# GpSimd's wait for TensorE's sum in the last group of a tile: ahead of the first gather instead of ahead of the fifth

## The reference

```
hh = (x @ W).reshape(n, 8, 32)                      # x is layer-normed
scores = leaky_relu(s_src[src] + s_dst[dst])        # 206250 edges, sorted by dst
e = exp(scores - m[dst]);  alpha = e / denom[dst]
out = segment_sum(hh[src] * alpha, dst)             # per node, 256 wide
x = x + elu(layernorm(out + x))
x = x + moe(layernorm(x))                           # top 2 of 16 experts, 256-512-256, layernorm
```

## Time and profile before

| | |
|---|---|
| median of three runs | 3359.55 us |
| span of the profiled execution, first to last instruction | 3356.0 us |
| edge loop, about 150 to 2740 us of the span | POOL busy 1558 us of 2590 |
| in it | DVE busy 1345, PE 1219, ACT 740 us |
| one gather | 0.948 us busy, next one 0.30 us later |

### The profile page before, as it was taken

How to read it: one execution, slowest core, us unless ns; L and a number is a source line. 1 busy time by engine, 2 the same in 40 slices (tenths; PEclk the granted TensorE clock), 3 DMA queues, 4 the chain that set the end, 5 groups by cost and what they waited for, 6 DMA issues and landing times. The chain is left out here.

```text
span 3356.0 us, 43456 instructions
## 1 busy us (share of the span) xinstructions
PE 1788.4 (53%) x9190; PEld 1461.1 (44%) x9191; DVE 1682.9 (50%) x3940; ACT 1018.8 (30%) x2031; POOL 1847.4 (55%) x1944
## 2 busy tenths in 40 slices
PE   6243544545444454544545444454544535999985
PEld 5133433434333343433434333343333434898974
DVE  7454554645445454554645545454554542333346
ACT  4232323233232332323223232332323312333442
POOL 2456656666565665656666565665656523555520
PEclk9676777767777776777777777777777767999987
DMA  5443434434343343443434343343433336333343
GB/s 185 115 122 96 123 112 113 118 105 122 105 123 117 105 119 105 124 115 107 119 105 124 106 121 115 107 120 102 125 117 107 118 82 202 101 102 102 106 158 120
DMA packets 179756, 393.55 MB, mean 117 GB/s; under 512 B 52144, under 2 KB 100576, under 8 KB 173448
## 3 DMA queue, kind: packets, MB, share of 16 engines
q0 software_dynamic: 93984, 273.52, 28.5%
q1 hardware_dynamic: 69512, 105.33, 10.1%
q10 hardware_dynamic: 16224, 14.30, 1.6%
HBM read 356.52 MB, written 36.47 MB: 117 GB/s over the span
## 5 line engine op out<-in xcount | busy, mean ns | idle before, releaser
L1265 POOL DMA_INDIRECT gat<-table,idx x1632 | 1546.7, 948 | 996.0 <-issue 448.7
L1362 PE MATMUL ps_sum<-msg,hot 128*128 128x264 f32 x3332 | 1075.0, 492 | 1051.4 <-DVE msg L1409 793.1
L1362 PEld LDWEIGHTS ps_sum<-msg,hot 128*128 128x128 f32 x3332 | 814.4, 250 | 1253.9 <-issue 1069.4
L1409 DVE TENSOR_TENSOR msg<-gat,ps_weight 128x2304 f32<-128x2304 f32 x196 | 473.4, 2415 | 401.3 <-ACT ps_weight L1321 392.5
L1560 DVE TENSOR_TENSOR num<-acc,ps_sum 128x264 f32<-128x264 f32 x49 | 21.0, 429 | 692.2 <-remote 681.2
L1277 ACT ACTIVATE hotT<-dst_row,neg_id 128x4352 bf16<-128x4352 int16 x48 | 188.3, 3922 | 283.1 <-remote 255.1
L1679 ACT ACTIVATE std<-var 128x1 f32<-128x1 f32 x49 | 9.9, 203 | 832.3 <-DVE var L1571 832.3
L1406 DVE TENSOR_TENSOR hot<-ps_own,rel 128x1152 f32<-128x1152 f32 x196 | 251.0, 1280 | 0.0
L1348 PE MATMUL ps_look<-dst_split,hotT 128*128 (+1 forms) x1666 | 80.2, 191 | 276.9 <-ACT hotT L1279 264.2
L2089 PE MATMUL ps_ht<-xT,w_t 128*128 128x128 f32 x1712 | 213.4, 278 | 3.6 <-issue 1.7
L2089 PEld LDWEIGHTS ps_ht<-xT,w_t 128*128 128x128 f32 x1712 | 201.8, 194 | 7.9 <-issue 4.3
(11 more groups left out here) (397 smaller groups left out, 2056.5 us busy)
## 6 DMA issues: line engine op xcount, KB each, us to landing
dst_row<-dst_half SPq DMA_DIRECT2D x49, 1088.0 KB
gat<-table,idx POOLq DMA_INDIRECT x1666
b_t<-in_L_ffn_b_dram ACTq DMA_DIRECT2D x107, 128.0 KB
w_sb<-in_L_ffn_w_dram SPq DMA_DIRECT2D x6, 2048.0 KB, 12.4
listing<-list_f SPq DMA_DIRECT2D x736, 0.5 KB
back<-chosen SPq DMA_DIRECT2D x5, 1792.0 KB, 7.6
table<-rows SPq DMA_DIRECT2D x49, 128.0 KB, 1.7
y_rows<-y SPq DMA_DIRECT2D x49, 128.0 KB
```

What stands on the lines that cost most here:

```text
L1265: pool.indirect_dma_start(gat[:, GSTART[g] + k, :], None, table, bass.IndirectOffsetOnAxis(ap=idx[g][:, k:k + 1], axis=0)).then_inc(landed ...
L1362: last = pe.matmul(ps_sum[:, 0:SUM], hot[:, m, k, :], msg[:, m, k, :], start=(g == 0 and k == 0), stop=(g == NG - 1 and k == n - 1))
L1409: dve.tensor_tensor(msg[:, m, 0:n, 0:D].rearrange("p j (h d) -> p j h d", d=HD), gat[:, j:j + n, 0:D].rearrange("p j (h d) -> p j h d", d=HD),
```

## The change

In g3 of every tile, GpSimd's wait for `sum_done` of g3 of the tile before stands ahead of the first of the eight gathers, where it stood ahead of the fifth. g0 to g2 keep theirs.

```diff
                     for k in range(GROUPS[g]):
-                        if k == GROUPS[g] // 2:
+                        if k == (0 if g == NG - 1 else GROUPS[g] // 2):
                             pool.wait_ge(sum_done, (t - 1) * NG + g + 1)
                             pool.sem_inc(pool_turn, 1)
                         pool.indirect_dma_start(gat[:, GSTART[g] + k, :], None, table,
```

## The result

The changed kernel is 0.4% faster: median 3347.42 us of 10 runs against 3359.34 us of 10 runs of the kernel before, ratio 0.9961, 95% interval 0.9944 to 0.9978. The forecast was 3421 us, slower. The profiled execution has a span of 3342.4 us, 13.6 less than before.

The account below looks back on a forecast made before the run. Bound: a chain of waits through g3's signal, held until GpSimd stops. Terms of -5.0, +3.65, +0.2, +5.2 and -2.9 gave about 1.3 us per tile, over 47 tiles 61 us: 3421 us, range 3270 to 3515.

Parts of the forecast that it names:

- step 5: SyncE's list DMAs crawl, so `dst_row` goes out late in every tile: `hotT` +5.2 us, g3's signal no longer held -2.9.
- Reading of the bound: VectorE's wait at each tile's start: g3's sum is signalled only once GpSimd stops, 3.0 us after its last gather's end.
- Step 1: Four gathers leave the time ahead of g3's signal, so VectorE goes on earlier: a gain of 5.0 us per tile.
- Rival (C): g3's signal comes when TensorE is done, whatever GpSimd does: +172, 3531 us; chance 0.13, shared with results beyond the forecast.
- Step 2: On GpSimd the four moved gathers run behind the tile's start with g0's first four: twelve in a row, costing nothing themselves.
- Step 3: g0's sum falls amid twelve gathers in a row, so its signal is held: a cost of 3.65 us per tile.
- Rival (B): g0's sum isn't held: 4.6 us less per tile, 3144 us, or 3250 with half of it; chance 0.10.
- Step 4: From g1's gathers through `hotT` to g3's sum, adding 0.2 us: a tile takes 51.8 us, 1.1 less than 52.9.
- rival (A): SyncE issues its lists and `dst_row` in time, so step 5 is void: -52, 3308 us; chance 0.25.
- (D): The terms cancel, or the moved wait is passed at once: time within 0.2%; chance 0.12.

Follow-up runs that it names:

- e3: The changed kernel with the wait for g3's sum at g3's third gather instead of the first: 3292.33 us (one run), against 3364.7 us for the kernel before.
- e7: e1 with the wait for g3's sum at g3's third gather instead of the first: 3266.84 us, ratio 0.970 to the kernel before.
- e11: e7 with GpSimd's wait for g3's sum taken out: 3650.68 us (one run), against 3391.13 us for the kernel before.
- e6: The kernel before with `dst_row` issued ahead of the lists and one of eight matmuls left in g3's sum: 3270.53 us (one run), against 3364.7 us.
- e1: The changed kernel with `dst_row` issued ahead of the 16 list DMAs instead of behind them: 3274.25 us, ratio 0.9675 to the kernel before.
- e2: The kernel before with only `dst_row` issued ahead of the list DMAs: 3387.0 us, ratio 1.0002.
- e12: e7 with GpSimd's waits for the sums of all four groups taken out: 3928.42 us (one run), against 3391.13 us for the kernel before.
- e5: The kernel before with gathers of g2 and g3 fetching 64 bytes a row instead of 1088: 3399.57 us (one run), against 3384.21 us.
- e8: e7 with a fill of a scratch tile on GpSimd ahead of g1's and g3's first gather: 3467.07 us, ratio 1.0318 to the kernel before.
- e9: e7 with a fill of a scratch tile on GpSimd ahead of g3's first gather alone: 3259.76 us, ratio 0.9695 to the kernel before.

## Why the prediction was wrong, point by point

The forecast was 61 us more, measured are 12 us less. The step that failed is step 5, the count of SyncE's lists; the others were right in kind, with sizes off by up to 1 us.

**Reading of the bound: right for this kernel, too narrow as a rule.** The sum's signal comes some 3 us after GpSimd stops: S + 14.3 with the wait at the fifth gather, S + 11.5 at the third (e3, e7), S + 8.7 at the first, S + 20.2 with none (e11). But the 3 us aren't fixed (the last section has the counts), and e6 has signals that are late with no stop at all.

**Step 1: right.** S + 9.2 was forecast, 8.7 measured: L1560 at 1051.22 with the stop at 1048.64, a gain of 5.6 us against 5.0, since 2.6 us lie between stop and L1560 and not 3.1. Rival (C) falls with it, with e3 and with e6.

**Step 2: right.** Twelve gathers run without a pause, 1001.38 to 1016.08, T + 15.4 as forecast.

**Step 3: right in kind.** g0's sum is held: L1703 at T + 17.7 in both tiles, forecast T + 18.55, T + 15.1 if not held. The fifth gather of g0 starts at T + 18.4 instead of T + 19.35, a cost of 2.7 us for 3.65. Rival (B) falls.

**Step 4: right.** `hotT` at T + 31.5 and S at T + 41.8, forecast T + 32.3 and T + 42.6. The first tile above takes 50.5 us, forecast 51.8 for a tile with `dst_row` in time: 0.5 us of that is step 1's, the rest step 3's.

**Step 5: wrong.** Its single tile was met: `dst_row` at T + 31.6 (forecast T + 33), `hotT` at T + 38.2 (37.5), S at T + 48.5 (47.9), T = S + 6.6 (6.3), a tile of 55.1 (54.2). What failed is that I let every tile be late. The step starts its count with 1 to 2 lists out before T, which holds where the sum is held up. But the late tile it arrives at ends with a prompt sum beside a quiet GpSimd, and there the lists go out 1.26 us apart and five are out before T. By the step's own count the next tile then has 5 + 6 + 2 to 3 + 4 = 17 or 18 lists of time for 16, and is in time, as measured: `dst_row` at T + 25.4. I had written this very argument for rival (A) and gave it 0.25 instead of carrying the late tile's end state into the next count. The mean of 50.5 and 55.1 is 52.8, 0.1 us below before, where the step had +1.3; over 47 tiles these 1.4 us are 66 of the 74 us between forecast and result. With the alternation, the prediction's own prices of 51.8 and 54.2 us give a mean of 53.0: so 1.2 of the 1.4 us are the step's error, and 0.2 are sizes that were off either way and partly cancel, which is luck. The 5.2 us ahead of the first L1560, which a sum over 47 tiles left out, are most of the rest.

**The rivals.** (A) priced a kernel in which SyncE is in time, 3308 us, 1.5% faster; e1, which makes it so, is 3.2% faster, so (A) was priced too high (on e1's chip a tile went from e2's 53.5 to 51.1 us, where (A) had 1.1 us less). The result lies between (A) and the forecast because the tiles do. (D), "the terms cancel", comes nearest to the time, though not within 0.2%.

## What to carry to other kernels

When a step's sum ends in a different state from the one it began with, it has to be run a second time from that state: the alternation would have come out of the prediction's own numbers, as 51.8 and 54.2 us and about no change (measured 50.5 and 55.1). When a change removes hundreds of us of waiting and the time hardly moves, look for the instruction whose idle time is new in the costliest groups; here it was one DMA queued behind sixteen small ones, and moving it turned 0.4% into 3.2%. Before a wait that protects nothing is taken out, ask what gets done while its engine stands still: here it cost 8 us per tile to remove one.

## What the hardware showed that was not expected

Beside unbroken gathers of GpSimd (one per 1.25 us), TensorE's signals reach VectorE, ScalarE and GpSimd late: in the kernel before and most others 2 to 5 us after GpSimd stops, in 13 of 45 tiles of e6 while it goes on. In e11 the signal of a 5.4 us sum comes 20.2 us after the sum's start, in its first tile 28.4 us. The delay is longer the longer GpSimd has gone without a pause. Counted over the tiles whose sum is held up until after the stop (a pause is over 0.6 us; the times are medians and run to L1560's start):

| gathers since the last pause | from stop to L1560, us |
|---|---|
| 13 | 2.6 (after), 2.8 (e1) |
| 15 | 2.8 (e7), 2.9 (e3) |
| 16 | 3.4 (e12) |
| 17 | 3.1 (before), 3.3 (e2) |
| 21 | 4.0 (e11) |
| 26 | 4.4 (before, first two tiles) |
| 30 | 5.2 (e11, first two tiles) |

Kernels with the same count differ by some tenths, and e12 stands above its neighbours; from 13 to 30 gathers the delay doubles. The prediction carried the 3.0 us of 17 gathers over to 13. The matmuls behind are recorded on time, and a sum with an eighth of the work is signalled as late behind the stop, 3.2 us (e6), so it is the signal and not the work. SyncE goes slow with it, 4.9 us per list instead of 1.2. The bytes moved play no part (e5), a pause of 0.90 us with at most four gathers behind it was enough for g0's sum (e3, e7), and a gap of the same length filled by other work was enough in one place and not in another (e8, e9).

The cause stays open. The Trainium skill, "NOTIFIC — the notification-queue block", section 7.1, says that a full path for event records can stall the producing engine. That would fit a delay that grows with the work since the last pause and that is seen in the records of every execution here, but nothing here shows it: an execution without records would have to be timed beside one with them.
